# Moving GpSimd's scatters of expert results ahead of the unit's other work in an attention and mixture-of-experts kernel

## What is computed

```
x = x + attention(layernorm(x), ctx) @ W_out + b_out
y = layernorm(x)
logits = y @ Wg.T + bg;   w = softmax of the two largest logits
gate, up = even and odd columns of  y @ Wgu[e] + bgu[e]
gate = min(gate, 7);   up = clip(up, -7, 7)
out_e = ((up + 1) * gate * sigmoid(1.702 * gate)) @ Wd[e] + bd[e]
x = x + sum over the token's two experts e of  w_e * out_e
```

## Time and profile before

| | |
|---|---|
| median of 3 runs | 596.6 us (596.18 to 596.95) |
| the profiled execution | 594.73 us |
| its span in the trace | 592.9 us (1.83 us lie around it) |
| mean granted TensorE clock | 0.969 of full speed |
| GpSimd's last scatter of results, start | 569.6 us |
| share of DMA in the last 22 us (571 to 593) | 0.88 |

### The profile page before, as it was taken

How to read it: one execution, slowest core, us unless ns; L and a number is a source line. 1 busy time by engine, 2 the same in 40 slices (tenths; PEclk the granted TensorE clock), 3 DMA queues, 4 the chain that set the end, 5 groups by cost and what they waited for, 6 DMA issues and landing times.

```text
span 592.9 us, 20076 instructions
## 1 busy us (share of the span) xinstructions
PE 521.4 (88%) x6712; PEld 445.6 (75%) x6712; DVE 521.9 (88%) x1496; ACT 481.5 (81%) x1364; POOL 464.1 (78%) x567
## 2 busy tenths in 40 slices
PE   2898999999999999999999999999866878999800
PEld 0577889898999998989898999998755656666600
DVE  5879999999999999999999999999998869877616
ACT  0897999999999999999999999999966565766600
POOL 8995766788898988989898898988884577777730
PEclk9998999999999999999999999999999898999965
DMA  9793165229306384930762393075503232333139
GB/s 272 203 319 69 14 196 194 46 51 331 91 11 180 86 264 135 325 87 12 211 209 45 66 327 88 13 230 189 120 20 83 68 90 82 105 91 96 48 128 315
DMA packets 69703, 81.64 MB, mean 138 GB/s; under 512 B 8116, under 2 KB 47564, under 8 KB 69604
## 3 DMA queue, kind: packets, MB, share of 16 engines
q1 hardware_dynamic: 56244, 67.60, 39.3%
q0 software_dynamic: 4352, 8.47, 4.3%
q10 hardware_dynamic: 9008, 4.30, 2.7%
HBM read 18.82 MB, written 46.31 MB: 110 GB/s over the span
## 4 chain that ended last, share of the span: by engine, by line
PE 71%; DVE 12%; ACT 6%; issue 5%; DMA 3%; ACTq 2%; POOL 0%; POOLq 0%; SPq 0%; DVEq 0%
PE bank L1385 17%; PE bank L1384 17%; PE bank L1386 16%; PE bank L1502 8%; PE bank L1550 5%; PE bank L1591 3%; DMA ctx_sb<-results 2%; ACTq L511 1%; ACT probs L612 1%; PE bank L1640 1%; DVE pT L1251 1%; PE bank L1624 1%; PE bank L1394 1%; PE bank L1529 1%; DVE qmax L1230 1%
## 5 line engine op out<-in xcount | busy, mean ns | idle before, releaser
L612 ACT ACTIVATE probs<-bank,nbias 128x128 f32<-128x128 f32 x512 | 146.0, 368 | 4.2
L1251 DVE TENSOR_TENSOR pT<-bank,pT 128x512 f16<-128x512 f32 x128 | 87.4, 683 | 9.1 <-ACT pT L631 6.6
L928 POOL DMA_INDIRECT results<-z,stage x72 | 71.2, 989 | 21.8 <-issue 13.4
L1230 DVE TENSOR_REDUCE qmax<-bank 128x4 f32<-128x512 f32 x128 | 87.0, 679 | 0.6 <-PE bank L1386 0.6
L1384 PE MATMUL bank<-keys,q_pad 128*128 128x128 f16 x480 | 86.6, 219 | 0.0
L1386 PE MATMUL bank<-keys,q_pad 128*128 128x128 f16 x480 | 86.6, 219 | 0.0
L1385 PE MATMUL bank<-keys,q_pad 128*128 128x128 f16 x480 | 86.6, 219 | 0.0
L814 POOL DMA_INDIRECT places<-payload,slots x64 | 65.8, 1029 | 22.5 <-issue 9.3
L1502 PE MATMUL bank<-ident,probs 128*128 128x128 f32 x512 | 78.3, 275 | 4.5 <-DVE pT L1251 3.9
L631 ACT ACTIVATE pT<-bank 128x512 f16<-128x512 f32 x128 | 78.1, 610 | 4.9 <-PE bank L1502 4.8
L1384 PE MATMUL bank<-xT,w_qkv 128*128 128x256 f16 x256 | 69.9, 273 | 1.1 <-DVE xT L974 0.8
(11 more groups left out here) (266 smaller groups left out, 1958.1 us busy)
## 6 DMA issues: line engine op xcount, KB each, us to landing
places<-z SPq DMA_DIRECT2D x8, 4160.0 KB, 14.9
q_pad<-q_nat SPq DMA_DIRECT2D x120, 128.0 KB, 2.4
stage<-places SPq DMA_DIRECT2D x64, 65.0 KB, 1.8
ctx_sb<-results SPq DMA_DIRECT2D x14, 256.0 KB, 4.7
ctx_sb<-in_ctx_dram ACTq DMA_DIRECT2D x4, 512.0 KB, 10.5
stage<-in_L_ffn_Wgu_dram SPq DMA_DIRECT2D x1, 2048.0 KB, 9.5
out_dram<-x_sb ACTq DMA_DIRECT2D x7, 256.0 KB, 5.8
stage<-in_L_xattn_W_qkv_dram SPq DMA_DIRECT2D x3, 512.0 KB, 6.3
```

Source lines behind the costliest of these rows:

```text
L612: last = nc.scalar.activation(probs[:, b, k, :], score_bank[b][:, k * P:(k + 1) * P], ACT.Exp, bias=nbias[:, b, k:k + 1], scale=exp_scale)
L928: nc.gpsimd.indirect_dma_start(out=results, out_offset=bass.IndirectOffsetOnAxis(ap=to, axis=0), in_=z[:, (q - 5) % NZ, t, :], in_offset=None,
L1230: nc.vector.tensor_reduce(qmax[:, r % 2, :], score_bank[r % 2][:, :].rearrange("p (h k) -> p h k", h=4), AX.X, ALU.max).then_inc(s["qmax_o ...
L1251: nc.vector.tensor_tensor(pT[:, r % 2, LO, :], pt_bank[:, :], pT[:, r % 2, HI, :], ALU.subtract).then_inc(s["pt_lo"], 1)
```

## The change

On GpSimd `send` is called ahead of the step for units below 12, and behind it for the others. Since units below 5 send nothing, it concerns units 5 to 11, steps (16, 6) to (17, 4), and 14 scatters. Nothing is added or removed on any engine, and the other engines' programs are the same.

```diff
--- before.py
+++ after.py
@@ -930,7 +930,17 @@
                             in_=z[:, (q - 5) % NZ, t, :], in_offset=None,
                             bounds_check=2 * TOK - 1, oob_is_err=False).then_inc(z_sent[(q - 5) % NZ], 16)
 
-            over_last(nothing, step, send, nothing)
+            AHEAD = 12
+
+            def send_ahead(q, u, i):
+                if q < AHEAD:
+                    send(q, u, i)
+
+            def send_behind(q, u, i):
+                if q >= AHEAD:
+                    send(q, u, i)
+
+            over_last(send_ahead, step, send_behind, nothing)
```

## The result

| | before | after |
|---|---|---|
| median | 596.55 us (594.14 to 597.54, 22 runs) | 598.38 us (21 undisturbed runs, 596.23 to 600.21) |
| ratio | | 1.003, interval 1.002 to 1.0041 |
| profiled execution, span | 594.73, 592.9 us | 598.99, 597.2 us |

Slower by 1.8 us, 0.3%: inside the range of 595.3 to 598.9, but not the 596.7, no change, that was forecast. The runs of the changed kernel also spread wider (standard deviation 1.15 us against 0.80), and the spread goes with TensorE's clock: the fastest (596.23) has a mean granted clock of 0.969, the slowest (600.21) of 0.962, and over the 21 runs the correlation of clock and time is -0.91. One further run at 606.02 us was disturbed and is left out.

What follows compares the result with a forecast made beforehand. GpSimd was taken as full for 101 us, PE's side close behind. GpSimd 1.5 us early meets `slots` 1.45 late: +0.12, tail +0.13, so +0.1 us, profiled 594.8, plus 1.9 to the median: 596.7 us, range 595.3 to 598.9.

Steps and rivals of the forecast that it cites:

- The path of the damage: Pair 15: scatters delay the shift 1.58 us, y slips 1.45, and the PE, ScalarE and VectorE round trip slips with it.
- The cover in front of that L814: At pair 15's first scatter on GpSimd: `slots` may slip 1.33 us (1.96 by the other value) before the scatter moves.
- The tail's cover: At block 36's scatter, the tail: z may come 1.32 us later (1.95 by the other value) before the end moves.
- the allowance for VectorE's interference: On the two early GpSimd scatters beside VectorE work: up to 2 x 0.42 = 0.84 us more delay, none at best.
- both start right behind the scatter that ends at 465.04: Block 0's two moved scatters on GpSimd: ready early enough to start at 465.34 instead of 470.04.
- GpSimd's own gain: Holes around the shift of pair 15: filling them brings GpSimd's later work forward by at most 1.5 us.
- the clock rival: TensorE after 470: longer PE idleness adds a low-clock stretch, +1.1 us, or +2.1 for two, 598.7 at worst; chance 0.17.
- From there both programs are the same, and GpSimd's pace sets 569.60 + 0.12: From pair 15's scatters to the last scatter: unchanged pace, so the end moves only by the +0.12 us at `slots`.
- My own case: Whole kernel: the y slip is nearly covered, +0.1 us, end moving -0.5 to +1.0; chance 0.52.

Runs made afterwards that it cites:

- g2: The changed kernel repeated unchanged, against the kernel before on the same chip: 597.97 against 595.94 us, ratio 1.0033.
- e3: The kernel before with two 128x1024 copies on ScalarE in front of y of pair 15, GpSimd untouched: 597.49 against 595.92 us, ratio 1.0028.
- e1: The changed kernel with only unit 5's two scatters in front, against the kernel before: 596.81 against 595.92 us, ratio 1.0015.
- g3: The changed kernel with unread matmuls on TensorE in the waits of units 7, 8, 9, against the kernel before: 596.58 against 595.94 us, ratio 1.0013.
- e2: The changed kernel with only units 6 to 11's scatters in front, unit 5's behind, against the kernel before: 597.64 against 595.92 us, ratio 1.0029.
- g4: Units 6 to 11 in front, unit 5 behind, timed again against the kernel before: 597.51 against 595.94 us, ratio 1.0020.
- f2: The changed kernel with only unit 11's two scatters in front of the copy L799, against the kernel before: 596.73 against 596.50 us, ratio 1.0004.
- g1: The kernel before repeated unchanged, against itself: 595.88 against 595.94 us, ratio 1.0006.
- f3: The kernel before with pair 15's copy L799 moved into GpSimd's hole in front of the shift: 596.34 against 596.50 us, ratio 0.9993.
- f4: Pair 15's copy L799 in the hole before the shift plus units 6 to 11 in front, against the kernel before: 596.63 against 596.50 us, ratio 1.0000.
- f1: The changed kernel with only units 6 to 10 in front, 5 and 11 behind, against the kernel before: 596.11 against 596.50 us, ratio 0.9993.

## Why the prediction was right or wrong

**What held.** The last scatter of results ends the stretch: in both profiles of the changed kernel every gap behind pair 15's first L814 is 0.30 or 0.31 us. The path of the damage was the one described, scatters, shift, y, then ScalarE and VectorE together, `slots`, pair 15's L814. The cover in front of that L814 exists: in g2 a slip of 1.9 us in `slots` moves it by 0.6. The tail's cover of 1.3 us exists too: in the changed kernel block 36's z is ready at 564.60, so its scatter could start at 565.38 (0.78 later), and it starts at 566.81.

```profile
564.24 0.62 ACT L663 ACTIVATE z<-bank,stage 128x128 f32<-128x128 f32 x2
```
```profile
566.81 0.98 POOL L928 DMA_INDIRECT results<-z,stage  x1 [0.30 <-issue]
```

So the delay of the last scatter came through the first L814 and the stretch behind it, not through the tail. Nor was the allowance for VectorE's interference needed: the two early scatters took 1.00 us each, with VectorE busy 1.97 of 2 us beside them (466 to 468), and 1.02 was reckoned.

**The step that failed first: "both start right behind the scatter that ends at 465.04".** The scatter waited for z, 0.78 us from its ready time. I had used the 0.77 us of a waiting scatter for the covers and forgot it for the first moved one. y slipped by 1.83 us, not 1.45; the cover of 1.33 then leaves 0.5, not 0.1. (The scatters held the shift's first instruction back by 2.19 us instead of 1.58, and 0.2 came back because the four small instructions took 1.55 us instead of 1.78.)

**GpSimd's own gain, "by at most 1.11 + 0.42 = 1.5 us", was too large.** The 0.42 was no hole: the L814 behind the shift stands 0.74 us behind it in the changed kernel as well. With the shift, one L814 and two scatters done, GpSimd comes to the next scatter 7.23 us after the start of z (472.29), where it came 7.93 after it before:

```profile
472.76 0.96 POOL L814 DMA_INDIRECT places<-payload,slots  x1 [0.30 <-issue]
```

That is 0.7 us gained, and the wait for z at 484.31 takes it back in the first profile (2.01 us; in g2 it is 0.57). It didn't matter for the end, since the L814 waited for `slots`.

**The clock was a rival with 0.17 and is a part of the likeliest case.** With y late and TensorE's waits unfilled the low-clock time between 468 and 486 was 3.4 us twice and 10.2 us twice (g2, e3; after, e1), and with y in time 0 in six profiles and 3.4 in two. The mean granted clock over the timed runs points the same way: 0.966 for g2, 0.971 for the kernel before on the same chip, 0.974 for g3. Filling PE's waits gave 1.4 us back by the medians (g2 to g3; interval 0.5 to 1.9), so PE's idleness behind the late y costs roughly that beyond the slip itself. The two profiles, g2's with one short low stretch, differ by 0.4 us at the last scatter. The rival's price, +1.1 us for one more low stretch and +2.1 for two, was of the right size; its chance was too small. The Trainium skill, "TensorE: Matmul & The Clock Gate", "Part 1: The HAM clock gate", says that idleness throttles TensorE, and g3 agrees: with PE busy 1.70 us of 470 to 472 instead of g2's 0.32 the granted clock stays at 1.00 up to 486, where g2's falls at 472.

**The term that was missing: "From there both programs are the same, and GpSimd's pace sets 569.60 + 0.12".** The programs are the same, the pace isn't. The stretch took 0.94 us more in the profiles in which the copy isn't followed by unit 11's scatter. I had costed the swap at unit 11 at nothing. It has a second price, the gap of 0.97 us between the copy and the L814 behind it: in the changed kernel it is hidden, because the L814 waits for `slots` anyway, in e2, g4 and f2 it shows and puts the L814 0.7 us later than in the two profiles of the kernel before.

**The sum by the table.** Changed kernel: first L814 later by 0.5 us (g2 against the mean of before and g1, 26.46) to 1.9 us (first profile), stretch longer by 0.94: +1.4 to +2.9 us, measured 1.8 and 2.0. Units 6 to 11 alone: 0.7 + 0.94 = 1.6, measured 1.7 and 1.2 to 1.6. Unit 5 alone, with the stretch as before: only the L814's part, 0.5 to 2.0, measured 0.9. The parts don't add up to the whole, since the late `slots` and the gap behind the copy stand side by side in front of the same L814. The sum sets places from single profiles against medians of timed runs and leaves out what lies behind the last scatter, so that it agrees but doesn't prove.

**Where luck comes in.** My own case ended at +1.0 us. The measured +1.8 lies in the stated range only because the clock rival and an allowance for VectorE stretched it to 598.9.

**What stays open.** f2, f3 and f4 were timed on a chip on which the longer stretch cost less than its 0.94 us or nothing, though their profiles show it (f3 and f4 measured -0.2 and +0.1 us by the medians). The chip alone doesn't lengthen the stretch: f1, on the same chip and with unit 11's order as before, has 78.80. The kernel before wasn't profiled there. Nor was it found why the place of a copy 0.2 us long should change the duration of sixty later scatters, or why the time behind the last scatter differs by up to 1.8 us between profiles.

## What to carry to other kernels

Before putting work into an engine's idle gap, look at what stands behind the gap: here the idle GpSimd was about to make two numbers per row, for which ScalarE and behind it VectorE and TensorE waited, and a hole of 1.1 us was no place for 2.3 us of scatters that were themselves not ready. A slip that a later queue would hide can still cost by what it does to TensorE's clock, so price the idle time that it makes on PE, not only the slip. And when moving DMAs on GpSimd, look at what comes to stand right behind a small operation: here an L814 came 0.97 us behind it, a scatter of results 0.17. That keeping them apart saves time on the whole wasn't shown (f3, f4).

## What the runs showed that I had not expected

- An indirect DMA on GpSimd that waits for the small copy just in front of it starts 0.97 us after its end (e2, f2, g4); one that doesn't wait for it, 0.17 us after (g1). But the wait isn't all of it, since the L814 behind the shift, which has no wait for it, starts 0.72 to 0.74 us after.
- The commonest distance of indirect DMAs issued back to back is 1.28 us in five profiles and 1.29 in nine, fixed for some 60 of them, and which one it is goes with whether unit 11's scatter follows the copy L799. No mechanism is shown.
- The same kernel with the same y ran one execution with 10.2 us at the low clock and one with 3.4, and the kernel before one with 3.4 and one with none: the low-clock time behind a gap in PE's work differs from execution to execution. It is a likely source of the wider spread of the changed kernel's runs, whose times go with their mean clock; other stretches at the low clock add to that mean, so this isn't shown.
- The time from the last scatter to the end is 23.3 to 25.1 us with the same instructions, in fourteen profiles.
